# One more buffer for the mixed probabilities, and the transposes one slot later

## The reference, cut to what matters

```
q = (x @ Wq)  -> 16 heads of 32;  k likewise;  v -> 8 heads of 64
dots = q k^T * 32**-0.5                       # 4 x 16 x 1024 x 1024
attn_w = softmax(dots)
attn_w = attn_w[:, :, 0] - lam * attn_w[:, :, 1]   # heads in pairs: 8 differences
attn = attn_w @ v
attn = gamma * attn / (rms(attn) + EPS) * (1 - LAMBDA_INIT)
x = x + attn @ Wout
```

## Time and profile before

| what | us |
|---|---|
| median of 3 runs | 1417.99 (1416.45 to 1418.41) |
| profiled execution | 1416.29 |
| its span in the trace | 1414.2 |
| PE, DVE, ACT, POOL busy in the span | 1238.8, 1186.1, 1046.3, 1094.1 |
| first part, units 0 to 255 on POOL | 41.8 to 1023.4 |
| granted PE clock, mean of the span | 0.966 of full speed |

### The profile page before, as it was taken

The page is one execution under the profiler, slowest core; times in us unless marked ns, Lnnn a source line. Parts: engine busy times, 40 slices in busy tenths (PEclk is TensorE's granted clock), DMA queues, the critical chain, the costliest instruction groups (busy, mean ns, idle before and its releaser), DMA issues. The chain is left out here.

```text
span 1414.2 us, 24279 instructions
## 1 busy us (share of the span) xinstructions
PE 1238.8 (88%) x8370; PEld 749.8 (53%) x8370; DVE 1186.1 (84%) x1969; ACT 1046.3 (74%) x1935; POOL 1094.1 (77%) x778
## 2 busy tenths in 40 slices
PE   2789999999999999999999999988851599999997
PEld 1444444444444444444444444444431588888897
DVE  5899999999999999999999999998757366767665
ACT  2798888888888888888888888888633365556553
POOL 3899999999999999999999999999933443434330
PEclk9799999999999999999999999999975799999999
DMA  4232111121111112111111211110021776868670
GB/s 111 71 89 61 38 44 51 36 66 41 51 51 31 51 42 61 40 51 51 31 53 44 65 31 51 30 31 1 1 50 24 136 126 109 146 106 141 106 130 10
DMA packets 184600, 86.87 MB, mean 61 GB/s; under 512 B 150176, under 2 KB 166048, under 8 KB 184480
## 3 DMA queue, kind: packets, MB, share of 16 engines
q1 hardware_dynamic: 184480, 85.33, 28.7%
HBM read 7.68 MB, written 2.10 MB: 7 GB/s over the span
## 5 line engine op out<-in xcount | busy, mean ns | idle before, releaser
L1233 DVE TENSOR_REDUCE negmax<-score_ps 128x1 f32<-128x1024 f32 x512 | 614.3, 1215 | 58.4 <-PE score_ps L601 56.4
L917 ACT ACTIVATE prob<-score_ps,negmax 128x1024 f32<-128x1024 f32 x512 | 569.5, 1115 | 102.8 <-DVE negmax L1233 101.2
L482 POOL TENSOR_TENSOR prob<-prob 128x1024 f32<-128x1024 f32 x256 | 603.4, 2357 | 21.4
L601 PE MATMUL score_ps<-ka,qa 128*128 128x512 f16 x1024 | 308.9, 384 | 41.9 <-ACT prob L917 28.4
L624 PE MATMUL trans_ps<-ident,prob 128*128 128x128 f32 x2048 | 283.1, 277 | 34.7 <-POOL prob L482 31.6
L624 PEld LDWEIGHTS trans_ps<-ident,prob 128*128 128x128 f32 x2048 | 232.9, 141 | 119.3 <-POOL prob L482 72.5
L480 POOL TENSOR_SCALAR prob<-prob,ccol 128x1024 f32<-128x1024 f32 x256 | 287.1, 1121 | 6.7 <-DVE ccol L1246 6.7
L630 PE MATMUL attn_ps<-probT,v_sb 128*64 128x512 f32 x1024 | 276.8, 620 | 1.1 <-DVE probT L326 1.1
L549 POOL TENSOR_TENSOR xs<-xnT,rw_all 128x2048 f32<-128x2048 f32 x32 | 115.5, 3609 | 168.9 <-DVE prob L1367 162.1
L846 ACT ACTIVATE probT<-trans_ps 128x512 f32<-128x512 f32 x256 | 153.8, 601 | 39.7 <-PE trans_ps L624 37.1
L326 DVE COPY probT<-trans_ps 128x512 f32<-128x512 f32 x256 | 174.1, 680 | 5.5 <-PE trans_ps L624 5.5
(11 more groups left out here) (194 smaller groups left out, 1283.4 us busy)
## 6 DMA issues: line engine op xcount, KB each, us to landing
qa<-split SPq DMA_DIRECT2D x256, 64.0 KB, 2.0
ka<-split SPq DMA_DIRECT2D x256, 64.0 KB, 2.0
xg<-xnT SPq DMA_DIRECT2D x16, 512.0 KB, 3.0
resid<-in_L_attn_x SPq DMA_DIRECT2D x4, 512.0 KB, 5.7
wg<-in_L_attn_Wkv SPq DMA_DIRECT2D x32, 64.0 KB, 2.0
out<-yo SPq DMA_DIRECT2D x32, 64.0 KB, 2.4
wg<-in_L_attn_Wq SPq DMA_DIRECT2D x16, 64.0 KB, 1.9
xsT<-prob SPq DMA_TRANSPOSE x64, 4.5
```

The source lines that it names most:

```text
L482: pool.tensor_tensor(prob1[:, u, :], prob1[:, u, :], prob2[:, u, :], ALU.add).then_inc(mix_ok, 1)
L601: mm = pe.matmul(score_ps[:, sub, kh * HALF:(kh + 1) * HALF], qa[:, par, head * 2 + sub, q0:q0 + P], ka[:, par, head * 2 + sub, kh * HALF: ...
L917: act.activation(prob2[:, s % 4, :] if sub else prob1[:, s % 4, :], score_ps[:, sub, :], ACT.Exp, bias=negmax[:, s % 2, sub:sub + 1], accu ...
L1233: dve.tensor_reduce(negmax[:, s % 2, sub:sub + 1], score_ps[:, sub, :], AX.X, ALU.max, negate=True).then_inc(max_ok, 1)
```

## The change

`prob1` and `ccol` get five buffers (PROBS), indexed by n modulo 5; `prob2` keeps four. TRANS_LAG goes from 3 to 4, and all lags that are reckoned from it go up by one with it: PV_LAG 12, PV_END and COPY_LAG 19, ROWS_LAG 20, STAT_LAG 21, ROOT_LAG 22, NORM_LAG 24, COLS_LAG 25, PROJECT_LAG 26, TAIL_SLOTS 29. PE's transposes in slot n so wait for the mix of unit n-4. ACT's first exp now waits for the transposes of unit n-5; its second waits as before. POOL's stream keeps its order: root and norm stand behind the mixes of units 4 and 5. In the fills, the v pieces move from slots 4 and 12 of a step to 3 and 11, and in the first step the q piece moves from 3 to 4, since rows, cols and project now fall in slots 4, 1 and 2 of each half. LN2_SLOT and the slots bound to it stay. `attnT` becomes another name for `attn_nT`, and its copy waits for the projection that read that tile; `yo` is put into the fifth buffer of `prob1`.

```
@@ -61,10 +61,11 @@
-TRANS_LAG = 3
+PROBS = 5
+TRANS_LAG = PROBS - 1
...
-PV_LAG = 11
+PV_LAG = TRANS_LAG + 8
@@ -75,12 +76,12 @@
-PROJ_SLOTS = {4: ("v1", 0), 5: ("k0", 1), 7: ("k1", 1), 12: ("v0", 1), 13: ("q0", 2), 15: ("q1", 2)}
+PROJ_SLOTS = {3: ("v1", 0), 5: ("k0", 1), 7: ("k1", 1), 11: ("v0", 1), 13: ("q0", 2), 15: ("q1", 2)}
...
-FIRST_SLOTS = {0: ("ln", 0), 1: ("ln", 1), 2: ("ln", 2), 3: ("q0", 1), 6: ("q1", 1), 8: ("ln", 3), 9: ("ln", 4), 10: ("ln", 5)}
+FIRST_SLOTS = {0: ("ln", 0), 1: ("ln", 1), 2: ("ln", 2), 4: ("q0", 1), 6: ("q1", 1), 8: ("ln", 3), 9: ("ln", 4), 10: ("ln", 5)}
@@ -178,12 +179,12 @@
-        prob1 = sb("prob1", [P, 4, T])
+        prob1 = sb("prob1", [P, PROBS, T])
...
-        x2sq = prob1
-        xs_split = prob1[:, :, :].bitcast(F16).rearrange("p (r n) (e c) -> p r n e c", r=2, c=C)
+        x2sq = prob1[:, 0:4, :]
+        xs_split = prob1[:, 0:4, :].bitcast(F16).rearrange("p (r n) (e c) -> p r n e c", r=2, c=C)
@@ -199,13 +200,13 @@
-        ccol = sb("ccol", [P, 4])
-        attnT = sb("attnT", [P, HALF])
+        ccol = sb("ccol", [P, PROBS])
...
+        attnT = attn_nT.rearrange("p t q -> p (t q)")
@@ -246,7 +247,7 @@
-        yo = sb("yo", [P, 2, C])
+        yo = prob1[:, 4, 0:2 * C].rearrange("p (r c) -> p r c", r=2)
@@ -477,9 +478,9 @@
-                pool.tensor_scalar(prob2[:, u, :], prob2[:, u, :], ccol[:, u:u + 1], 1.0, ALU.mult, ALU.mult).then_inc(scaled_P, 1)
+                pool.tensor_scalar(prob2[:, n % 4, :], prob2[:, n % 4, :], ccol[:, u:u + 1], 1.0, ALU.mult, ALU.mult).then_inc(scaled_P, 1)
...
-                pool.tensor_tensor(prob1[:, u, :], prob1[:, u, :], prob2[:, u, :], ALU.add).then_inc(mix_ok, 1)
+                pool.tensor_tensor(prob1[:, n % PROBS, :], prob1[:, n % PROBS, :], prob2[:, n % 4, :], ALU.add).then_inc(mix_ok, 1)
@@ -506,7 +507,7 @@
-                    mix(8 * h + u, u % 4)
+                    mix(8 * h + u, (8 * h + u) % PROBS)
@@ -621,7 +622,7 @@
-                                mm = pe.transpose(trans_ps[:, kb, t * P:(t + 1) * P], prob1[:, u % 4, k0:k0 + P], ident[:, :])
+                                mm = pe.transpose(trans_ps[:, kb, t * P:(t + 1) * P], prob1[:, (n - TRANS_LAG) % PROBS, k0:k0 + P], ident[:, :])
@@ -910,11 +911,11 @@
-                        if sub == 0 and not (first and s < 4):
-                            act.wait_ge(trans_ok, 2 * (n - 3))
-                        if sub == 1 and not (first and s < 4):
+                        if sub == 0 and n >= PROBS:
+                            act.wait_ge(trans_ok, 2 * (n + 1 - PROBS))
+                        if sub == 1 and n >= 4:
...
-                        act.activation(prob2[:, s % 4, :] if sub else prob1[:, s % 4, :], score_ps[:, sub, :], ACT.Exp,
+                        act.activation(prob2[:, n % 4, :] if sub else prob1[:, n % PROBS, :], score_ps[:, sub, :], ACT.Exp,
@@ -956,7 +957,7 @@
-                            act.wait_ge(rows_ok, 4 * it + half)
+                            act.wait_ge(out_ok, 4 * it + half)
@@ -1239,11 +1240,11 @@
-                        half, u = ((s - 1) // 8) % 4, (s - 1) % 8
+                        half, u, c = ((s - 1) // 8) % 4, (s - 1) % 8, (n - 1) % PROBS
...
-                        dve.tensor_scalar(ccol[:, (s - 1) % 4:(s - 1) % 4 + 1], recip2[:, r:r + 1], sums[:, half, 0, u:u + 1],
+                        dve.tensor_scalar(ccol[:, c:c + 1], recip2[:, r:r + 1], sums[:, half, 0, u:u + 1],
```

## The result

| | before | after |
|---|---|---|
| time, median of 10 runs each | 1416.45 us (1416.02 to 1418.41) | 1420.62 us (1419.40 to 1422.61) |
| ratio, 95% interval | | 1.0027 [1.0018, 1.0035] |
| profiled execution, its span | 1416.29, 1414.2 | 1420.87, 1418.7 |
| POOL, DVE busy | 1094.1, 1186.1 | 1094.1, 1218.3 |

The change makes the kernel 0.27% slower, some 4 us. The forecast was +0.8 us and 1418.8 us. The sign came out, and so did most of the mechanism; the size didn't.

A forecast was written before the change was run, and what follows sets the result against it. POOL was taken to set the rate. Steady halves 0, start +1.6, fills 0 and tail -0.8 gave +0.8 us, and from the median of 1417.99 a time of 1418.8 us; range 1415.0 to 1424.0.

The forecast's parts named there:

- The bound: Loop: POOL sets the rate, 3.55 us from one add to the next; PE's waits for the mix don't count.
- the steady halves at 0: Later halves of the loop: POOL's work and order stay, so the period of 30.7 us stays; cost 0.
- The held scaling: DVE's 128x8 scaling L1273 is held until POOL's running add ends, some 2 us in later halves.
- M: End of POOL's add of unit 3 of a half; DVE's reciprocal due at M + 8.26, POOL wanting it at M + 8.42.
- The start, +1.6: First half's norm: 1.8 us gained up to unit 20, then L1273 held in slot 21; norm 1.56 us later.
- Slots 22 and 23 have a gap more, +1 us: Upper bound of the start: a further gap in these two slots adds 1 us; start 0 to +2.6.
- PE's idle time as cover: Fills: PE has 11.6 of 200 us to spare, and DVE's 2 us stop at L1273 hides a late PE.
- The tail, -0.8: Behind the last unit: POOL's 2.00 us wait before the centring goes, the third sum costs 1.2; norm 0.8 us earlier.
- The fills and the tiles at 0: Moved q and v pieces and renamed tiles: number and sizes stay, attnT's projection is done already; cost 0.
- Rival (A): Every half: POOL's norm waits 0.21 us for L1252 behind the held L1273; +5.9 us, 1424.7 us; chance 0.23.
- Rival (B): Start: the front end's lead works there and L1273 is not held; 3.7 us faster, 1414.3 us; chance 0.13.
- Rival (C): ACT's second exp keeps its wait for unit n-4, so the queue isn't longer; start and tail 0, 1418.0; chance 0.16.

The follow-up runs named there:

- the second profile: The changed kernel run once more, unaltered, with a second profiled execution: 1420.37 us, 1.0026 against the kernel before.
- the last experiment: The changed kernel with the scaled row sums on ACT and the root and norm of half 0 one unit later: 1417.86 us, 1.0000.
- the first experiment: The changed kernel with the first step's fills as before (q piece in slot 3, v piece in slot 4): 1419.68 us, 1.0027.

## Why the prediction was right, and where its size was off

- **The bound, and the steady halves at 0: right for the first profile.** 891.01 us against 891.05 over 29 halves. PE's waits for the mix fell and bought nothing. In the second profile three halves cost 1.44 us together.
- **The held scaling: right.** It was forecast from a single row, and it is pinned to the end of POOL's add in a late half just as worked out: L1276 at M - 0.07 (forecast M - 0.06), the reciprocal done and handed over at 527.35 + 0.19 + 0.08 = M + 8.25 (forecast M + 8.26), the norm at M + 8.40 (forecast M + 8.42). The hold itself was put at some 2 us and has a median of 1.36.
- **The start, +1.6: the term that was mis-sized.** It measured +4.16 in the first profile and +1.54 in the second (125.72 - 124.18). The first splits in two against the forecast: unit 20 came at 115.38 and not at 113.89, 1.49 us, with a late rise of PE's clock in that execution; and from unit 20 to the norm it took 12.96 us and not 11.85, 1.11 us, about the size of the gap of 1.04 us behind the fallen clock. In the second profile the two are -0.64 and +0.62, so its agreement with the forecast's 1.56 is luck: an early rise of the clock hid the term that was missing. "Slots 22 and 23 have a gap more, +1 us" stood in the bounds, without its mechanism: DVE is held, so PE idles, so PE's clock falls, so DVE gets a second gap. I had counted PE's idle time as cover. That is the step that failed. The firm evidence is the distance from unit 20 to the norm: 8.45 to 8.47 us in all five profiles with the lag of 3, 12.47 to 12.96 in four with the lag of 4 and the hold, 10.17 with ACT's scaling. That edit takes away the hold, most of PE's stall and the fall of the clock together; that the clock makes the second gap is read from the rows and not separated by a run.
- **The tail, -0.8: wrong, it is 0 in the first profile.** The centring did start without its wait, but the root of half 30 didn't gain 2.0 us with it. It hangs on that half's own products from PE (ACT's copy at L936, then DVE's L1276) and moved up by 4.12 - (1034.67 - 1031.36) = 0.81 us only (1031.36 is the root's start before). Then all three sums stood before the reciprocal: from root to reciprocal 2.90 us against 2.04, 0.86 lost. Net 0.05. One profile can't say more: the way from the loop's last norm to the last residual addition is 35.78 us in both profiles of before, but 34.63 in one with the same tail; with the changed tail it is 35.84 and 35.33 in the two profiles of after.
- **The fills and the tiles at 0: right as far as tested,** 0.9997 for the first step's fills and 1.0003 for the buffers and tiles. The moved v pieces of the later steps have no run of their own, but the last experiment keeps them and reaches 1.0000.
- **Rival (A), the hold as a bound in every half:** not in every half, but it exists. It shows in single halves when PE's clock dips behind the hold: 0.91, 0.21 and 0.32 us in one profile, 0.65 and 0.81 in another, 0.96 in a third. **Rival (B)** would have needed an early unit 20 and no hold; the first came, the second not. **Rival (C)** is out: DVE's busy time and the transposes' wait both changed.
- **Sum.** 0 + 4.2 + 0 + 0 in the first profile, against 0 + 1.6 + 0 - 0.8; in the second 2.8 + 1.5 + 0 - 0.5.
- **The time: right in part by luck.** The 1418.8 was reckoned from a median of three runs, 1417.99; over ten runs the same kernel's median is 1416.45. These 1.5 us of the base brought the forecast nearer to 1420.62 than its step of +0.8 did. The measured step is about +4.2, five times as large.

What stays open: what sets the instant at which PE's clock rises (46 and 54 us in two executions of the same code, 50 in both of before); why a half takes 30.72 us in some executions and 30.77 in others, with either lag; why an idle PE comes back at half its clock in one half and at full clock in most; and how often the late waits come. They are why two profiles of the same kernel reach about the same span, 1418.7 and 1418.0, by different routes, and why the split of the 4 us holds for an execution and not for the median. Also open: with ACT's scaling the kernel before stands at 0.9983 and the one after, with its first norm later, at 1.0000. No profile explains that remaining 0.17%: the profiled execution of the latter was its slowest, with PE's clock rising at 55 us and halves of 30.78 us.

## What to carry to other kernels

When a DVE scaling on SBUF operands, as the one here, is moved against a POOL that never rests, look at where in POOL's instruction it will start, and price the hold until that instruction's end, however small it is. Then follow the hold through the queue: the engine that idles behind it may come back at half its clock, as PE did here. The cheapest cure was to give the small instruction to an engine that isn't held (ACT, here 0.17% from either kernel), and a longer lag for an engine that isn't the bound buys nothing.

## What the runs showed of the hardware

- A DVE scaling of 128x8 took 0.16 us, or 1.36 us (median of after) when it started inside a POOL add of 2.36 us; in the first experiment's profile it took up to 2.18. It ended 0.01 to 0.04 us behind the add. The Trainium skill says in "SBUF — State Buffer", "Who interferes with whom", that a DVE instruction in a two-port mode and a GpSimd instruction exclude each other: the one that issues first has the shared ports to its end, and the other is blocked. The trace agrees, at a size of 8 elements a partition. The RECIPROCALs and the reductions among the same rows were not lengthened (0.15 to 0.20 us, 0.67 us).
- An idle stretch of PE of 2.02 us took its granted clock from 1.00 to 0.50, and eight transposes from 1.04 to 1.92 us; where the hold was gone (idle 0.67 us) the clock stayed at 1.00 in the same place. After an idle stretch of 1.83 us in one profile the clock fell as well, after one of 1.76 us in another it didn't.
- The same code saw the clock at 1.00 from 46 us in one execution and from 54 us in another; unit 20 moved by 2.1 us with it.
